# Graph attention's edge passes: transposes, sums and the accumulator one visit further behind, sums first in TensorE's visit

## The reference, cut to what matters

```
m     = xl[src] + xr[dst] + edge_attr @ We.T
score = where(m > 0, m, 0.2 * m) @ att
smax  = segment_max(score, dst);  es = exp(score - smax[dst])
out   = segment_sum(es / denom[dst] * xl[src], dst)
```

## Time and profile before

| what | value |
| --- | --- |
| median of three runs | 7688.16 us |
| the profiled execution's own time | 7706.77 us |
| its span, first to last instruction | 7704.8 us |
| mean granted TensorE clock in it | 0.867 |
| first edge pass, visits from 165 to some 3045 us | 2880 us |
| second edge pass, visits from 3161 to some 5997 us | 2836 us |

### The profile page before, as it was taken

One profiled execution on the slowest core, in us unless ns is written; L12 is line 12 of the kernel. 1 busy time (PEld: TensorE's weight loads), 2 busy tenths in 40 slices (PEclk: granted clock), 3 DMA queues, 4 the chain that ended last, 5 costly groups with the idle time before them and its releaser, 6 DMA issues. The chain is left out here.

```text
span 7704.8 us, 170425 instructions
## 1 busy us (share of the span) xinstructions
PE 5782.3 (75%) x40520; PEld 4186.0 (54%) x40521; DVE 4089.8 (53%) x12731; ACT 2572.1 (33%) x4831; POOL 3042.2 (39%) x3157
## 2 busy tenths in 40 slices
PE   3777777777777776577777777777777698999699
PEld 2555555555555554455555555555555683222689
DVE  6455555555455555555555555555555527778532
ACT  2233333333333332333333323333333205777210
POOL 3555555555555553455555555555555000000000
PEclk9888888888888887788888888888888898999899
DMA  3333222232232332332332332332332362323479
GB/s 83 73 77 75 69 77 70 75 77 69 75 77 71 79 77 49 76 82 70 77 78 69 78 77 70 80 76 69 79 79 64 148 270 76 134 105 109 172 295 362
DMA packets 689323, 764.63 MB, mean 99 GB/s; under 512 B 368995, under 2 KB 574026, under 8 KB 664145
## 3 DMA queue, kind: packets, MB, share of 16 engines
q1 hardware_dynamic: 561781, 577.66, 24.5%
q0 software_dynamic: 100352, 102.96, 6.9%
q10 hardware_dynamic: 27102, 82.91, 2.8%
HBM read 671.04 MB, written 88.81 MB: 99 GB/s over the span
## 5 line engine op out<-in xcount | busy, mean ns | idle before, releaser
L336 POOL DMA_INDIRECT gat_rows<-rows_scr,gat_idx x3136 | 3015.6, 962 | 2862.7 <-PE gat_aps L1299 1237.0
L1290 PE MATMUL gat_tps<-ident,gat_weights 128*128 128x128 f32 x3136 | 601.2, 322 | 1319.3 <-ACTq L1155 1193.1
L1290 PEld LDWEIGHTS gat_tps<-ident,gat_weights 128*128 128x128 f32 x3136 | 384.1, 159 | 1508.1 <-ACTq L1155 1324.3
L1172 ACT ACTIVATE adj_tiles<-gat_counts 128x392 f32 (+1 forms) x784 | 390.8, 498 | 2161.2 <-remote 1135.1
L1308 PE MATMUL gat_sps<-gat_relu,gat_att 128*128 128x256 f32 x3136 | 1079.9, 478 | 0.0
L1071 DVE CUSTOM_DVE_ANT_0 gat_masked<-gat_sps,gat_miss,gat_oldtop 128x512 f32<-128x512 f32 x784 | 586.9, 749 | 754.6 <-remote 462.5
L1022 DVE TENSOR_SCALAR adj_hot_key<-adj_iota_key,adj_winbase,adj_key 128x392 bf16<-128x392 int16 x2416 | 960.5, 398 | 8.7 <-issue 8.7
L1299 PE MATMUL gat_aps<-gat_rows,gat_weightsT 128*128 128x65 f32 x6224 | 955.7, 306 | 0.0
L1299 PEld LDWEIGHTS gat_aps<-gat_rows,gat_weightsT 128*128 128x128 f32 x6224 | 938.5, 231 | 0.0
L1063 DVE COPY gat_oldtop<-gat_top 128x1 f32 x784 | 119.6, 153 | 1334.7 <-issue 622.2
L1021 DVE TENSOR_SCALAR adj_hot_lo<-adj_iota_lo,adj_low 128x128 bf16<-128x128 int16 x2416 | 636.9, 264 | 266.5 <-issue 108.4
(11 more groups left out here) (379 smaller groups left out, 6837.8 us busy)
## 6 DMA issues: line engine op xcount, KB each, us to landing
gcn_sum_adj<-adj_scr SPq DMA_DIRECT2D x98, 1568.0 KB, 8.5
gat_dstb<-dst_scr SPq DMA_DIRECT2D x784, 128.0 KB
gat_ea<-in_ea SPq DMA_DIRECT2D x784, 128.0 KB
gin_sum_adj<-adj_scr SPq DMA_DIRECT2D x49, 1568.0 KB, 8.5
adj_scr<-adj_tiles ACTq DMA_DIRECT2D x48, 1568.0 KB
at_adj<-adj_scr SPq DMA_DIRECT2D x60, 1024.0 KB, 9.5
gat_rows<-rows_scr,gat_idx POOLq DMA_INDIRECT x3136
gat_xr<-xr_scr SPq DMA_DIRECT2D x1568, 24.0 KB
```

What stands on the lines that cost most here:

```text
L336: pool.indirect_dma_start(ring.rows[:, u, c, 0:ROW], None, rows_d, bass.IndirectOffsetOnAxis(ap=ring.idx[:, u, c:c + 1], axis=0)).then_inc ...
L1290: last = pe.transpose(tps[:, c * P:(c + 1) * P], wts[:, j, c * P:(c + 1) * P], ident[:])
```

## The change

The transposes move from two visits behind to three, the sums from three to four, the accumulator from four to five. The sums go from behind the transposes to the very start of TensorE's visit. ScalarE's copy of the transposes follows by one visit (its place in the visit stays). VectorE gets a further wait, on `weight` of four visits before, ahead of the masking, and carries one more block number; `shrink` is indexed for five behind. A fifth drained accumulator step is added, and the drained exponentials and copies are re-numbered. The core of the diff:

```diff
-    delay = {..., "turned": 2, "evac": 2, "sum": 3, "acc": 4, "topped": 3, "olded": 2}
+    delay = {..., "turned": 3, "evac": 3, "sum": 4, "acc": 5, "topped": 3, "olded": 2}
...
                     dve.wait_ge(s["topped"], count("topped", step, 3))
-                    dve.wait_ge(s["sum"], count("sum", step, 4))
+                    dve.wait_ge(s["sum"], count("sum", step, 5))
...
                     dve.wait_ge(s["score"], count("score", step, 2))
+                    dve.wait_ge(s["weight"], count("weight", step, 4))
...
-                j = (u - 2) % 2
-                act.wait_ge(s["turned"], count("turned", step, 2))
-                act.wait_ge(s["sum"], count("sum", step, 4))
+                j = (u - 3) % 2
+                act.wait_ge(s["turned"], count("turned", step, 3))
+                act.wait_ge(s["sum"], count("sum", step, 5))
                 act.activation(wtsT[:, j, :], tps[:], ACT.Copy).then_inc(s["evac"], 1)
...
+                    j = (u - 4) % 2
+                    if not (first and u < 4):
+                        pe.wait_ge(s["evac"], count("evac", step, 4))
+                        pe.wait_ge(s["acc"], count("acc", step, 5))
+                        for c in range(GC):
+                            last = pe.matmul(aps[:, 0:D + 1], wtsT[:, j, c * P:(c + 1) * P], ...)
+                        last.then_inc(s["sum"], 1)
 
                     v, j = slot + u, u % 2
                     pe.wait_ge(s["masked"], count("masked", step, 0))
...
-                    j = (u - 2) % 2
-                    pe.wait_ge(s["weight"], count("weight", step, 2))
-                    pe.wait_ge(s["evac"], count("evac", step, 3))
+                    j = (u - 3) % 2
+                    pe.wait_ge(s["weight"], count("weight", step, 3))
+                    pe.wait_ge(s["evac"], count("evac", step, 4))
                     for c in range(GC):
                         last = pe.transpose(tps[:, c * P:(c + 1) * P], ...)
                     last.then_inc(s["turned"], 1)
-
-                    j = (u - 3) % 2
-                    if not (first and u < 3):
-                        pe.wait_ge(s["evac"], count("evac", step, 3))
-                        pe.wait_ge(s["acc"], count("acc", step, 4))
-                        for c in range(GC):
-                            last = pe.matmul(aps[:, 0:D + 1], wtsT[:, j, c * P:(c + 1) * P], ...)
-                        last.then_inc(s["sum"], 1)
```

More of the change, by code:

```diff
@@ L812, in gat_edges @@
     s = {n: k.sem(f"{tag}_{n}") for n in names}
-    delay = {"masked": 0, "message": 0, "fifth": 0, "relu": 1, "score": 1, "top": 2, "weight": 2, "turned": 2, "evac": 2,
-             "sum": 3, "acc": 4, "topped": 3, "olded": 2}
+    delay = {"masked": 0, "message": 0, "fifth": 0, "relu": 1, "score": 1, "top": 2, "weight": 2, "turned": 3, "evac": 3,
+             "sum": 4, "acc": 5, "topped": 3, "olded": 2}
     s_loaded = k.sem(tag + "_loaded")
@@ L1119, in _ @@
                 turn(i + TAIL // TURN, False)
-            for u in range(DRAIN):
+            for u in range(CARRY):
                 drained(u)
@@ L1148, in visit @@
                 j = (u - 2) % 2
[L1149 to L1155, removed]
+                if not drained or u < 2:
+                    act.wait_ge(s["top"], count("top", step, 2))
+                    act.wait_ge(s["turned"], count("turned", step, 4))
+                    act.activation(wts[:, j, :], masked[:, j, :], ACT.Exp, bias=newtop[:, j:j + 1], scale=-1.0)
+                    act.wait_ge(s["acc"], count("acc", step, 6))
+                    act.activation(shrink[:, (u - 2) % 4:(u - 2) % 4 + 1], oldtop[:, (u - 2) % 4:(u - 2) % 4 + 1], ACT.Exp,
+                                   bias=newtop[:, j:j + 1], scale=-1.0)
+                    act.drain().then_inc(s["weight"], 1)
                 if not drained:
@@ L1318, in _ @@
             behind = pe.alloc_register(tag + "_pe_behind")
[L1319 removed]
+            pe.reg_mov(behind, ODD - 4)
             with pe.Fori(0, tails) as i:
[L1321 removed]
+                visits(i * TURN + TAIL, TURN, i + WOVEN, False, back=pe.snap(behind, min_val=ODD - 4, max_val=RING - 4),
                        slot=ODD)
[L1323 removed]
+                pe.reg_mov(behind, RING - 4)
             for u in range(DRAIN):
                 step = tails * TURN + (TAIL + u)
+                j, v = (u - 4) % 2, ODD + u
+                pe.wait_ge(s["evac"], count("evac", step, 4))
+                pe.wait_ge(s["acc"], count("acc", step, 5))
+                for c in range(GC):
+                    last = pe.matmul(aps[:, 0:D + 1], wtsT[:, j, c * P:(c + 1) * P], rows[:, v, c, 0:D + 1],
+                                     start=(c == 0), stop=(c == GC - 1))
+                last.then_inc(s["sum"], 1)
+                if u < 3:
+                    j = (u - 3) % 2
+                    pe.wait_ge(s["weight"], count("weight", step, 3))
+                    pe.wait_ge(s["evac"], count("evac", step, 4))
+                    for c in range(GC):
+                        last = pe.transpose(tps[:, c * P:(c + 1) * P], wts[:, j, c * P:(c + 1) * P], ident[:])
+                    last.then_inc(s["turned"], 1)
                 if u == 0:
```

53 lines of the change are left out of this document (19 added, 34 removed).

## The result

The changed kernel takes 7849.31 us (median of 4 runs, 7830.56 to 7864.22), the kernel before beside it on the same chip 7690.36 us (4 runs). The ratio is 1.0207, 95% interval [1.0181, 1.0232]. The profiled execution took 7847.57 us, its span is 7845.6 us: 140.8 more than the 7704.8 of before. The prediction was 7412, so 276 us faster, with a range up to 7760: the kernel became slower instead, and its time lies outside the range.

A forecast was written before the change was run, and what follows sets the result against it. The prediction took a chain of waits, with a pause after gathers, to bound the kernel. Gains of 240 and 75 us less 39 made 276 us, from 7706.77 to 7431, shown as a median of 7412; range 7190 to 7760.

The forecast's parts named there:

- What bounds the kernel: In the two edge passes: a chain of waits, no full engine; all but TensorE pause some 3 us after gathers begin.
- 126 doubles: Estimated count of visits where eight gathers go out in a row, with a pause of 8.5 us; others issue four.
- Transposes three behind: In TensorE's visit with eight gathers: weights are already posted, so transposes fill the 7.12 us gap; part of 240 us gain.
- Sums first in the visit: At TensorE's visit start: copy and accumulator come in time, so next messages start 2.4 us earlier; 1.9 taken, 240 us total.
- Short waits: TensorE's 296 us of short waits for ScalarE's drain: most return as waits for VectorE's accumulator; a quarter, 75 us, gained.
- The added wait on VectorE: Before VectorE's masking: the wait never blocks but costs 50 ns a visit, 39 us in all.
- Queues that the moved step passes: GpSimd's ring slots, SP's refills and ScalarE's exponentials: enough lead remains, so each costs nothing.
- Slower: more doubles: Rival at GpSimd's wait for sums: earlier sums cause a quarter more eight-gather runs; 218 us slower, 7906 us; chance 0.21.
- No change: Rival: VectorE's work and the pause are the true cycle, TensorE only waits elsewhere; 7688 us; chance 0.10.
- What would show it: Signs: TensorE's drain wait under 300 us, GpSimd's sum wait down 100 to 300; much more VectorE "remote" before masking refutes.

The follow-up runs named there:

- halved runs: Kernel before and changed kernel, each without two of the four gathers a visit: 0.7608 and 0.813 of the kernel before with pauses, 0.9755 and 0.9337 without.
- acc_first: Changed kernel with VectorE's accumulator step moved to the start of VectorE's visit: 1.0126 of the kernel before.
- transposes_second: Changed kernel with transposes directly behind the sums, ahead of the messages, and ScalarE's copy first in its visit: 0.9911 of the kernel before; 0.9996 without pauses.

## Why the prediction was wrong, point by point

**What bounds the kernel.** Right: a chain of waits, with a pause of some 3 us in it, which GpSimd's gathers bring on. The halved runs show that (1848 us less). Missed: on what it hangs that TensorE runs through the pause of a single visit. It saw the 3.00 of 3.00 us; nothing that TensorE needed there came from an engine that stood, and the change ended that. The estimate of 126 doubles was good: the count is 128 pairs.

**"Transposes three behind."** Right about the wait: that for the drain went from 1193.1 us to nothing. But it gained nothing measurable (1.0021, 0.9974), as GpSimd then waits for the loads. Whether it costs something by itself stays open, as said under the added wait.

**"Sums first in the visit."** This is the step that failed. It says that "ScalarE's copy can follow its 0.38 us at 1810.60" and lies before 1811.9. That was worked out for the double alone, where everything starts at once when the pause ends. In the single visits, 488 of them against 128 pairs, no cost was worked out. There the copy can come only after the pause, in the visit shown 4.65 us after the transposes (1795.85 to 1800.50), and the sums and the gathers with it. Of its 240 us of gain some 145 came, and not as worked out: 43 pairs fewer, and those of eight gathers shorter by 1.07 us (16.60 to 15.53) where it took 1.9. The 302 us that the singles lost had no term.

**"Short waits."** It saw that the wait would come back at the start of the visit, but named the accumulator. By an own count of the 583 gaps of over 0.3 us in front of the sums, the copy came last in 340 (917 us) and the accumulator in 243 (386 us); acc_first and transposes_second bear out that ranking. And it bounded the loss by the 296 us that were there before, though a wait at another place has no reason to keep the old size: it is 1307.6 us.

**"The added wait on VectorE."** Expected to cost 39 us; alone it gave 0.9915, and 1.0003 on a chip without pauses. No cost was seen.

**"Queues that the moved step passes."** The ring slots lead far enough, as said. The copy that the sums wait for was not among the queues weighed: on ScalarE it stands behind the fifth, which waits for messages that now stand behind the sums. The DMA loads of SP, called "nothing", are the next wait as soon as the sums are on time (1169.9 us).

**The rivals.** "Slower: more doubles" (7906 us) had the side right and the mechanism wrong: pairs fell from 128 to 85. "No change" had the fault that waiting only moves; here it moved onto the one engine that had been free of the pause. The Trainium skill ("Perfetto Trace Analysis", Identifying the Most-Contended Engine) says to optimize the engine with the highest occupancy first, from which the prediction drew that nothing moves when no engine loses work. The trace doesn't agree: TensorE is at 75% in both kernels, and 2% lie between them.

**"What would show it."** VectorE's "remote" wait in front of the masking went from 462.5 us (114 times) to 1354.5 (358 times), but read as "the doubles grew" it misled. The pauses mostly met VectorE at another instruction, the read of the old maximum, before the change, and meet it at the masking since. Two lines of before, and the same two of after:

```profile
DVE gat_oldtop L1063 <- issue: 622.2, 331, 5.0
DVE gat_oldtop L1063 <- remote: 545.4, 220, 8.8
...
DVE gat_oldtop L1064 <- issue: 88.4, 92, 4.5
DVE gat_oldtop L1064 <- remote: 3.8, 1, 3.8
```

With the 161.5 and 137.4 us of "issue" in front of the masking, the "remote" and "issue" waits at the two places sum to 1792 us before and 1584 after. Over all of VectorE's instructions in the passes they sum to 2388 and 2516 us: 128 more, not the 892 that the one line suggests. GpSimd's wait for sums, expected to shrink by 100 to 300, grew by 688, in part because waits changed their label, as said under the result.

## What to carry to other kernels

Where a pause or any other common stall hits most engines, see which engine runs through it, and on what its next instruction depends: an order that puts it behind something from a stalled engine stops it too. Work out a moved step in each kind of visit of the timeline and weigh by their counts, instead of only in the one that the change goes for. And close the ring: follow the moved step's input back until it comes to the step itself, and count how many visits the ring has.

## What the runs showed of the hardware that was not expected

- **The pauses are not everywhere.** The kernel before took 7690 to 7753 us in five measurements and 5934 and 5930 in two, and the six with a chip on record (all but the first) were on six different chips. In those two no wait of VectorE, ScalarE or SP is marked "remote" (in before it was 462.5 us in front of VectorE's masking alone), and the clock is granted at 0.96. What causes it, the chip itself or something about it at the time, was not settled. The order of the steps is worth 2% on the one kind and, in the orders that were tried there with all gathers, nothing on the other. What holds the engines was not found either. It isn't the loading of instructions as far as the trace has it: none of the 88 packets of that kind in the kernel before lies between 250 and 2940 us, in the midst of the first pass.
- **The pause grows with the run of gathers, and faster than it.** It is some 3 us with four gathers and 8.5 us with eight, and with two VectorE is hardly held (2.9 us of "remote" in front of the masking in the whole kernel). Half of the gathers take 24% off where there are pauses, 2.5% where there are none.
- **ScalarE is held by a run of two gathers already,** for some 1.4 us past the end of its input (1.47 less 0.06) in the changed kernel; the mean of its waits for the messages is 2.38 us (1590.0 / 669) against 0.89 (502.1 / 562) without pauses, also some 1.5 us more.
- **The same change cost 2.07, 3.07 and 2.05% in three measurements with pauses.** So a difference of 1% between ratios from two measurements says nothing; what is compared above is from one chip, or said not to be.
- **A wait that is nearly always met made the kernel 0.85% faster** [0.9884, 0.9947] on one chip. It was not repeated where there are pauses, and neither was the 0.9911 of transposes_second, so whether either beats the kernel before stays open beyond those chips.
